# Scratch copies of four weight quarters: rows of 4096 bytes in padded rows, or rows of 2048 bytes chunk by chunk

## What is computed

```python
x = x + L0_ffn(L0_cond(x))      # x: 64 x 64 x 1024
x = x + L1_ffn(L1_cond(x))

L0_cond: x @ w_eff.T            # weight quantised to a 64 entry codebook, plus a low-rank delta
L0_ffn:  x @ W_base.T + b_base + sum over the top 2 of 8 experts of w_e * (x @ A_e.T) @ B_e.T * 2
L1_cond: x @ weight.T + bias + scale[a] * (x @ la[a].T) @ lb[a].T    # adapter a chosen by sequence
L1_ffn:  x @ base_W.T + sum over the top 2 of 8 experts of w_e * (x @ A_e) @ B_e * 2
```

## Time and profile before

| | us |
|---|---|
| median of 3 runs | 912.09 (911.99 to 912.55) |
| the profiled execution, its own time | 914.59 |
| its span, first to last instruction | 912.8 |
| PE busy | 904.0, 99% of the span |
| DVE busy | 616.2, 68% |
| ACT busy | 312.7, 34% |
| POOL busy | 145.3, 16% |
| mean granted TensorE clock | 0.997 of full speed |

### The profile page before, as it was taken

How to read it: one execution, slowest core, us unless ns; L and a number is a source line. 1 busy time by engine, 2 the same in 40 slices (tenths; PEclk the granted TensorE clock), 3 DMA queues, 4 the chain that set the end, 5 groups by cost and what they waited for, 6 DMA issues and landing times.

```text
span 912.8 us, 13364 instructions
## 1 busy us (share of the span) xinstructions
PE 904.0 (99%) x4672; PEld 789.1 (86%) x4672; DVE 616.2 (68%) x1311; ACT 312.7 (34%) x502; POOL 145.3 (16%) x298
## 2 busy tenths in 40 slices
PE   8999999999999999999999999999999999999998
PEld 8999998888998878888888888888888788888886
DVE  6789899776587959976465566566566566566563
ACT  6579788411224424232322222222222222212220
POOL 0100010111001001414213113113113113113110
PEclk9999999999999999999999999999999999999999
DMA  8523330665612032556887887887887887887875
GB/s 338 189 95 122 119 124 24 234 210 190 141 50 93 4 135 90 212 217 226 277 277 253 285 272 259 286 270 260 286 269 261 285 267 260 290 266 263 286 226 182
DMA packets 63090, 191.51 MB, mean 210 GB/s; under 512 B 10664, under 2 KB 13100, under 8 KB 61104
## 3 DMA queue, kind: packets, MB, share of 16 engines
q1 hardware_dynamic: 52448, 159.19, 50.8%
q0 software_dynamic: 10432, 31.35, 11.4%
q10 hardware_dynamic: 144, 0.13, 0.1%
HBM read 158.93 MB, written 32.23 MB: 209 GB/s over the span
## 4 chain that ended last, share of the span: by engine, by line
PE 88%; DMA 7%; DVE 3%; ACT 1%; issue 0%; SPq 0%; DVEq 0%; ACTq 0%
PE bank L852 26%; PE bank L518 13%; PE bank L519 13%; PE bank L520 13%; DMA t_lo<-t_scratch 5%; PE bank L826 5%; PE bank L835 5%; PE bank L663 2%; PE bank L909 2%; PE bank L923 2%; PE bank L922 2%; PE bank L924 2%; PE bank L580 1%; DMA x_raw<-xq 1%; DMA m_raw<-m1t 1%; DMA w<-e_scratch 1%
## 5 line engine op out<-in xcount | busy, mean ns | idle before, releaser
L852 PE MATMUL bank<-g_hi,xs 128*128 128x512 f32 x448 | 145.2, 395 | 0.0
L852 PE MATMUL bank<-t_hi,xs 128*128 128x512 f32 x336 | 113.4, 396 | 1.6 <-DMA t_lo<-t_scratch 1.4
L489 POOL DMA_DIRECT2D p1sel<-p_scratch x128 | 65.3, 510 | 280.2 <-issue 280.2
L852 PEld LDWEIGHTS bank<-g_hi,xs 128*128 128x128 f32 x448 | 83.2, 188 | 16.5
L954 ACT ACTIVATE xs<-x_raw 128x1024 fp32r<-128x1024 f32 x60 | 62.0, 1056 | 81.3 <-PE bank L852 55.7
L852 PE MATMUL bank<-g_lo,xs 128*128 128x512 f32 x224 | 88.3, 394 | 0.0
L1277 DVE TENSOR_TENSOR xs<-x_raw,xs 128x1024 fp32r<-128x1024 f32 x60 | 75.2, 1274 | 17.2 <-ACT xs L954 16.7
L518 PE MATMUL bank<-gx,xs 128*128 128x304 f32 x256 | 77.4, 302 | 0.0
L520 PE MATMUL bank<-gx,xs 128*128 128x304 f32 x256 | 77.4, 302 | 0.0
L519 PE MATMUL bank<-gx,xs 128*128 128x304 f32 x256 | 77.3, 302 | 0.0
L852 PEld LDWEIGHTS bank<-t_hi,xs 128*128 128x128 f32 x336 | 62.0, 188 | 16.6 <-DMA t_lo<-t_scratch 4.4
(11 more groups left out here) (321 smaller groups left out, 2064.2 us busy)
## 6 DMA issues: line engine op xcount, KB each, us to landing
t_hi<-t_scratch SPq DMA_DIRECT2D x82, 512.0 KB, 4.5
t_lo<-t_scratch SPq DMA_DIRECT2D x82, 512.0 KB, 5.9
x_raw<-xq SPq DMA_DIRECT2D x16, 1024.0 KB, 6.9
out<-ost SPq DMA_DIRECT2D x64, 256.0 KB, 4.7
p1sel<-p_scratch POOLq DMA_DIRECT2D x64, 192.0 KB, 4.7
w_raw<-wall SPq DMA_DIRECT2D x16, 512.0 KB, 4.3
w<-e_scratch SPq DMA_DIRECT2D x6, 1024.0 KB, 5.1
ea<-e_scratch POOLq DMA_DIRECT2D x8, 644.0 KB, 4.2
```

The costliest lines, as they stand in the source:

```text
L489: pool.dma_start(f(p1sel[b][STK * s:STK * s + STK, cs]), p1_dram[bass.ds(i * STK, STK), cs]).then_inc(sems[b], 16)
L852: mm = nc.tensor.matmul(bk[j][:], l[:, c, :], m[:, c, :], start=first and c + k == 0, stop=c + k == KH + 1, skip_group_check=True)
```

## The change

The scratch tensor is laid out by chunk. It was (4 quarters, 2 halves, hi and lo, 128 partitions, 1160); it is (4 quarters, 2 halves, hi and lo, 2 chunks, 128 partitions, 512). A partition's share of a half is no more one row of 4096 bytes, but two rows of 2048 bytes that lie 256 KB apart, and the rows of neighbouring partitions touch: the pitch falls from 4640 to 2048 bytes. The three places that name the tensor follow: the stores, the loads and the single reading back of T2. Everything else stands as it was: the same DMAs, of the same bytes, in the same order, with the same waits on every engine; SP's list has 318 rows before and after, and in 180 of them the shape reads 128x2x512 in place of 128x1024 (82 loads of each part, 8 stores of each); for T2 the shape was 128x2x512 before.

```diff
             def store_t(k, n):
                 for h in range(2):
                     sp.wait_ge(t_lo_s, 2 * n + h + 1)
-                    sp.dma_start(t_dram[k - 1, h, 0, :, 0:D].rearrange("p (c n) -> p c n", n=512),
+                    sp.dma_start(t_dram[k - 1, h, 0].rearrange("c p n -> p c n"),
                                  f(t_hi[:, 2 * h:2 * h + 2, :])).then_inc(st_t[h], 16)
-                    sp.dma_start(t_dram[k - 1, h, 1, :, 0:D].rearrange("p (c n) -> p c n", n=512),
+                    sp.dma_start(t_dram[k - 1, h, 1].rearrange("c p n -> p c n"),
                                  f(t_lo[:, 2 * h:2 * h + 2, :])).then_inc(st_t[h], 16)
 
             def load_t(k, used):
                 for h in range(2):
                     sp.wait_ge(t_free, used + h)
                     sp.dma_start(f(t_hi[:, 2 * h:2 * h + 2, :]),
-                                 t_dram[k - 1, h, 0, :, 0:D].rearrange("p (c n) -> p c n", n=512)).then_inc(ld_t[h], 16)
+                                 t_dram[k - 1, h, 0].rearrange("c p n -> p c n")).then_inc(ld_t[h], 16)
                     sp.dma_start(f(t_lo[:, 2 * h:2 * h + 2, :]),
-                                 t_dram[k - 1, h, 1, :, 0:D].rearrange("p (c n) -> p c n", n=512)).then_inc(ld_t[h], 16)
+                                 t_dram[k - 1, h, 1].rearrange("c p n -> p c n")).then_inc(ld_t[h], 16)
...
                     sp.dma_start(f(g[:, 2 * h:2 * h + 2, 512:D]),
-                                 t_dram[1, h, hl, :, 0:D].rearrange("p (c n) -> p c n", n=512)).then_inc(ld_t2, 16)
+                                 t_dram[1, h, hl].rearrange("c p n -> p c n")).then_inc(ld_t2, 16)
...
-    args.append(nc.dram_tensor("t_scratch", (4, 2, 2, P, NM1), F32, kind="Internal").ap())
+    args.append(nc.dram_tensor("t_scratch", (4, 2, 2, 2, P, 512), F32, kind="Internal").ap())
```

## The result

The changed kernel is slower by 0.31%: a median of 915.18 us over 11 runs (913.12 to 918.14) against 912.09 us over 11 runs of the kernel before, ratio 1.0031 with a 95% interval of 1.0017 to 1.0045. The ratio is the figure to go by; it makes 2.8 us, the two medians alone 3.1. The forecast was 912.4 with a range of 909.8 to 917.0: the time lies inside, but it is a time of the rival of the dearer loads (914.8 to 917.6), not of the likeliest case. The profiled execution has a span of 913.5 us, only 0.7 more than before's 912.8, because its streaming stages begin 1.7 us earlier, at 434.64 us in place of 436.35; the reason is told with the first experiment.

The account below looks back on a forecast made before the run. PE, busy 99%, bounds the kernel; scratch loads cost only 3.3 us of waits at T4's and T3's deadlines. Load delay adds 0.2 to 0.3 us, issues, stores and T2 about nothing: 912.09 + 0.3 = 912.4 us, range 909.8 to 917.0.

Parts of the forecast that it names:

- the rival of the dearer loads: T4's burst and T3's behind it: rows of 2048 are dearer in a full queue, 914.8 to 917.6 us; chance 0.31.
- the likeliest case: Whole kernel: loads cost about the same, 912.4 us, own range 910.3 to 913.9; 0.51 including the case of nothing cut.
- The cap on a gain: Streaming stages: all of PE's wait for scratch loads today, 3.3 us or 0.36% of the time, the most faster loads bring.
- Packets: SP's queue: 180 DMAs of 128 more rows each add 23,040 packets, 52,448 becoming about 75,500; bytes stay.
- the rival that nothing is cut: DMA engines cut rows at 2048 anyway: packets stay at 52,448, time 912.1 us; chance within the 0.51 for no change.
- The sum over the landings: T4's and T3's last parts: delay added to 14 landings each, excess past the deadlines summed; +0.2 to +0.3 us forecast.
- d: Delay of T4's last part behind its 2 MB burst: between -0.3 and +0.28 us, taken near 0 with 0.15 either way.
- The deadlines of 11.1 and 20.5: Microseconds after stage start by which T4's and T3's last parts must land; T3's shifts by what the stage already lost.
- T2's half at 4.7 us: T2's first half, 1 MB in pieces of 2048, complete 4.7 us after first issue, against T3's 4.86 with rows of 4096.
- the block at 5.0: A 1 MB block from `e_scratch`, one DMA of 512 rows of 2048, takes 5.0 us against 4.86 with rows of 4096.
- SP's issue time: SP's issues of T4's loads: cut loads take slightly longer to issue, 0.05 us at most, hidden by DMA work ahead.
- Stores and T2: Stages 0 and 1 and T2's read-back: no product waits for the stores, T2 has 10 us of cover; both at 0.

Follow-up runs that it names:

- the first experiment: The kernel before itself, unchanged, timed once more under another name against the kernel before: ratio 1.0003 (0.9995 to 1.0012), 911.83 us.

## Why the prediction was right, and where it wasn't

*What bounds the kernel.* Right. In the streaming stages PE waits for T4's and T3's last parts and for no other transfer, before and after: 1.4 us on PE before, 2.9 after, 5.3 with rows of 1024. The cap on a gain, 3.3 us, was never put to the test.

*Packets.* Right to the packet, and with it the rival that nothing is cut fell.

*The sum over the landings.* Right in form. It gives +2.1 us at T4 and +0.6 at T3 for d = 0.28, and with the measured d = 0.24 some +2.3; the two profiles gave +2.4, the timed runs +2.8. The deadlines of 11.1 and 20.5 held. One sign did not come: I had said that the dearer rows would show in 12 or more stages that are too long. Of the 13 full stages 6 are 0.3 us or more too long, against 5 before, though their excess is larger; 12 of 13 appeared only with rows of 1024.

*The size of d.* This is the term of the sum that was too small. I took d near 0, the middle between T2's half at 4.7 us and the block at 5.0, each against 4.86. In the two profiles it was 0.24, close to the upper end of 0.28 that I had worked out from the block; with the same rows in the old blocks the mean landing was 11.1, a d of 0.1 only, so the size is not firm. That the upper end of my own bracket came near is in part luck: single transfers outside the burst, one record each as I used them, decided between two values 0.3 us apart for a burst in a full queue. The row that did speak of a full queue, 394 against 421 GB/s at the same share, pointed the right way, and I gave it to the rival at 0.31.

*The layout.* I argued that the pitch holds nothing back, since rows at the old pitch reach 421 GB/s, and asked only whether a new layout could be faster. That it could be slower was not among my cases. Uncut rows in other places cost 0.14 to 0.28%. So part of what I booked as the price of cut rows is likely the price of leaving the old addresses. How the 0.31% divide is not settled: dense rows alone give 0.27, with old blocks 0.14; a further row each gives 0.13 or 0.14 where it could be read; but the changed kernel is only 0.04 above uncut dense rows. The two need not add. Nor is it shown by a trace how uncut rows elsewhere lose their time: the profiles of those kernels have 1.5 to 1.9 us of waits on PE, within or little above the spread of the kernel before (1.1 and 1.4 in its two).

*Where it arises.* I put the price into T4's burst. With T4 alone cut the ratio was 1.0006, and its interval excludes the 1.002 to 1.003 that this asked for. By the middle values the loads of T1 and T3 carry about two thirds. PE feels it at T4's and T3's deadlines; that the delay is gathered in the queue from all cut loads fits this, but the intervals don't show it.

*SP's issue time.* I allowed 0.05 us at most and called it hidden. It was 0.10 at T4's last part, and the padded cut rows, at 0.52 us an issue, show that it is not always small.

*Stores and T2.* Right: no wait for them appeared. *The range* held the time; the chance of slower by over 0.2% was 0.31, and too low.

## What to carry to other kernels

Where PE meets a load at its deadline in half of the stages, count how far each landing is from the deadline and sum what a small delay costs: by that sum a quarter of a microsecond in T4's and T3's last loads is worth 2.3 us here, 0.25%, while every busy share stays the same. Price a change to a transfer from rows in a queue as full as the one it will run in, and take the layout in DRAM as a cost of its own, of unknown sign: try the new rows with the old placement and the old rows with the new. Time the unchanged kernel once more under another name before believing a few tenths of a per cent, and compare executions of the same granted clock.

## What the runs showed of the hardware

- Kernels with uncut loads of the same bytes at four placements in DRAM (pitch 4640; 4096 with two block spacings; 4864) differ by up to 0.28% in time (0.18 to 0.31% where executions of the same clock are compared), the aligned and the dense ones being the slower. I had expected no difference or a gain.
- An issue of a hi part on SP takes 0.32 us for one row per partition, 0.38 for two rows 256 KB apart and 0.52 for two rows 2320 bytes apart; of a lo part, issued right behind it, 0.43, 0.47 and 0.61.
- DMA engine time for the same bytes: 50.8 to 51.5% of the span with rows of 4096, 50.7 to 51.7 with dense rows of 2048, 52.1 with padded ones, 53.4 with rows of 1024. Only the last stands clear of the spread between profiles.
- A load isn't shielded by its place in SP's queue: with 0.5 MB moved from ahead of T4's loads to behind them the first half landed 1.1 us earlier and the last part no earlier. With none, two and four stores of 256 KB behind, the last part followed the first half by 2.9, 3.5 and 4.6 us.
- The granted clock was 0.62 and 0.52 in the stretches from 10 to 14 us of the kernel before's profile, after two idle times of PE of 0.8 and 1.0 us, and 1.00 in the changed kernel's after idle times of 0.95 and 0.9: the streaming stages began 1.7 us later in the former. No run shows what decides between the two.
